# A fused stage's tail: a loop on PE for twelve groups, eight staging buffers, tables and paddings issued among them

## The reference, cut to what matters

```
x = x + tanh(g_xattn[0]) * attention0(layernorm(x), ctx)     # 16 heads
x = x + tanh(g_ffn[0])   * mixture_of_experts(layernorm(x))  # router, top 2 of 8 experts
Kp, Vp = ctx @ Wk + bk, tanh(ctx @ Wv + bv)                  # layer 1's keys and values
x = x + tanh(g_xattn[1]) * attention1(layernorm(x), Kp, Vp)
x = x + tanh(g_ffn[1])   * quantised_ffn(layernorm(x))
```

## Time and profile before

| what | value |
|---|---|
| three runs | 1030.18, 1034.2, 1043.85 us; median 1034.2 us |
| the profiled execution | 1035.45 us |
| its span, first to last instruction | 1033.6 us |
| granted clock of TensorE, mean | 0.840 of full |
| PE busy | 782.8 us (76%) |
| DVE, ACT, POOL busy | 731.4, 636.4, 610.2 us |
| DMA over the span | 132.16 MB, mean 128 GB/s |

### The profile page before, as it was taken

How to read it: one execution, slowest core, us unless ns; L and a number is a source line. 1 busy time by engine, 2 the same in 40 slices (tenths; PEclk the granted TensorE clock), 3 DMA queues, 4 the chain that set the end, 5 groups by cost and what they waited for, 6 DMA issues and landing times. The chain is left out here.

```text
span 1033.6 us, 19711 instructions
## 1 busy us (share of the span) xinstructions
PE 782.8 (76%) x6656; PEld 607.2 (59%) x6656; DVE 731.4 (71%) x1656; ACT 636.4 (62%) x1290; POOL 610.2 (59%) x617
## 2 busy tenths in 40 slices
PE   5389999988899889461499999999952798355355
PEld 3267767766676677350388888887741576322144
DVE  4776777877678874123287777777734798779988
ACT  5366666666667645251277777776741677489583
POOL 2145446878788886732057677776673884198500
PEclk9698988988889987785699999999985798767656
DMA  8123411122121214566667767676728533100013
GB/s 225 45 72 78 91 32 68 59 75 102 59 76 57 78 68 131 164 209 137 183 221 242 248 245 247 243 246 219 247 79 267 185 112 100 37 1 0 1 51 113
DMA packets 103827, 132.16 MB, mean 128 GB/s; under 512 B 23840, under 2 KB 78576, under 8 KB 97712
## 3 DMA queue, kind: packets, MB, share of 16 engines
q1 hardware_dynamic: 90240, 110.64, 33.8%
q0 software_dynamic: 9120, 18.91, 5.2%
q10 hardware_dynamic: 4368, 1.34, 0.9%
HBM read 86.59 MB, written 44.18 MB: 127 GB/s over the span
## 5 line engine op out<-in xcount | busy, mean ns | idle before, releaser
L1740 POOL DMA_INDIRECT m_results<-e_y,e_to x156 | 169.3, 1085 | 92.1 <-ACT e_y L1779 50.6
L324 POOL TENSOR_TENSOR a_probs<-a_probs,a_top 128x1024 f32<-128x1024 f32 x64 | 121.9, 1905 | 103.3 <-DVE a_top L958 100.6
L356 POOL DMA_INDIRECT m_tokens_to<-r_rows,r_place x128 | 128.4, 1003 | 46.5 <-issue 33.7
L1755 ACT ACTIVATE e_h<-e_ps_h,e_bias 128x512 f32<-128x512 f32 x156 | 107.6, 699 | 50.5 <-PE e_ps_h L1801 38.7
L1845 DVE TENSOR_TENSOR e_hp<-e_h,e_hp 128x512 fp32r<-128x512 f32 x156 | 108.2, 694 | 5.4
L1843 DVE CAST e_hp<-e_h 128x512 fp32r<-128x512 f32 x156 | 71.4, 458 | 52.9 <-ACT e_h L1755 38.4
L911 DVE TENSOR_TENSOR a_probs<-a_ps_s,a_mask 128x1024 f32<-128x1024 f32 x64 | 78.0, 1219 | 26.7 <-PE a_ps_s L548 26.2
L673 PEld LDWEIGHTS a_ps_o<-a_vals,a_probs_t 128*64 128x64 f32 x2048 | 74.6, 152 | 28.3 <-issue 27.7
L439 ACT ACTIVATE a_gated<-a_ps_o,tanh_gates 128x128 f32<-128x128 f32 x64 | 23.4, 365 | 101.3 <-PE a_ps_o L677 43.5
L673 PE MATMUL a_ps_o<-a_vals,a_probs_t 128*64 128x18 f32 x2048 | 81.4, 223 | 2.8 <-ACT a_heads_t L450 2.2
L694 PE MATMUL a_ps_pt<-ident,a_probs 128*128 128x128 f32 x512 | 81.6, 313 | 0.0
(11 more groups left out here) (291 smaller groups left out, 2018.3 us busy)
## 6 DMA issues: line engine op xcount, KB each, us to landing
e_weights<-m_weights_to SPq DMA_DIRECT2D x39, 1024.0 KB
e_rows<-m_tokens_to SPq DMA_DIRECT2D x39, 264.0 KB
a_ctx_in<-in_ctx_dram SPq DMA_DIRECT2D x32, 256.0 KB
m_weights_to<-r_parts SPq DMA_DIRECT2D x8, 1024.0 KB, 5.0
c_two<-m_results SPq DMA_DIRECT2D x3, 1536.0 KB, 15.3
m_keys_t<-n_keys SPq DMA_DIRECT2D x16, 256.0 KB
m_values<-n_values SPq DMA_DIRECT2D x16, 256.0 KB
c_keys_t<-m_keys_t SPq DMA_DIRECT2D x16, 256.0 KB, 2.6
```

Of the source, the lines that this page charges most:

```text
L324: pool.tensor_tensor(probs[:, j], probs[:, j], top[:, j].unsqueeze(2).broadcast_to([P, HEADS, SEQ]), ALU.subtract).then_inc(shifted, 1)
L356: pool.indirect_dma_start(tokens_to, bass.IndirectOffsetOnAxis(ap=place[:, k, q:q + 1], axis=0), rows[:, c % RING, q % CT, k, :], None).th ...
L1740: pool.indirect_dma_start(results, bass.IndirectOffsetOnAxis(ap=to[:, v, r:r + 1], axis=0), y[:, v, r], None).then_inc(sent[v], 16)
L1755: act.activation(h[:, c], ps_h[c][:], ACT.Gelu_apprx_tanh, bias=bias[:, n % ROWS, c:c + 1]).then_inc(h_sb, 1)
```

## The change

- The hand-written slots go. Contexts 0 to 3 stand in slots t = 64 to 67, the keys and values of groups 0 to 2 in slots 65 to 67. Groups 3 to 15 follow after the last slot: on PE the contexts 4 to 15 and the keys and values 3 to 14 in a `Fori` loop of three turns with four groups each, whose waits are computed from the loop's register; on ACT, DVE and SP as straight code.
- `keys1` and `values1` have eight buffers each, laid over `spread` and `probs`, and the waits for a store's landing are for the store eight groups earlier.
- On DVE `ends` is converted directly after the last places, then groups 3 to 5, then the tables, then groups 6 to 15.
- All eight paddings are issued by SP, one after the stores of each group from v = 5 on; ACT issues none.

```
@@ shapes @@
-    keys1 = sb("n_keys1", [P, 2, ST], F32)
-    values1 = sb("n_values1", [P, 2, QUAD, DM], F32)
+    keys1 = spread[:].rearrange("p u k t -> p (u k) t")
+    values1 = probs[:].rearrange("p j (h k) c -> p (j h) (k c)", h=2)
...
-    NEXT_SLOTS = (65, 66, 67, 69, 70, 71, 74, 75, 76, 78, 79, 80, 81, 82, 83, 84)
+    UNROLLED = 4
...
-        return NEXT_SLOTS.index(t) if t in NEXT_SLOTS else None
+        return t - TILES if TILES <= t < TILES + UNROLLED else None
@@ sync @@
             store_keys(v)
             if v:
                 store_values(v - 1)
+            e = v - UNROLLED - 1
+            if e == 0:
+                sp.wait_ge(ends_ready, 1)
+            if there(e, EXPERTS):
+                padding_of(sp, e)
         store_values(SUPERS - 1)
-        sp.wait_ge(ends_ready, 1)
-        for e in range(0, EXPERTS, 2):
-            padding_of(sp, e)
@@ scalar @@
-            if v >= 2:
-                act.wait_ge(keys_out[v % 2], 16 * (v // 2))
-            act.activation(keys1[:, v % 2], band(1), ACT.Identity, bias=bk1[:, 0:1]).then_inc(k1_sb, 1)
+            if v >= STAGED:
+                act.wait_ge(keys_out[v % STAGED], 16 * (v // STAGED))
+            act.activation(keys1[:, v % STAGED], band(1), ACT.Identity, bias=bk1[:, 0:1]).then_inc(k1_sb, 1)
...
+        for w in range(UNROLLED, SUPERS):
+            next_context(w)
+            next_keys(w - 1)
+        next_keys(SUPERS - 1)
         tanh_values(SUPERS - 1)
-        act.wait_ge(ends_ready, 1)
-        for e in range(1, EXPERTS, 2):
-            padding_of(act, e)
@@ tensor @@
+        def next_context(w, b, first=False):
+            if isinstance(w, int):
+                pe.wait_ge(loaded[b], 16 * ((SUPERS + w) // CTX_RING) + 16)
+            else:
+                pe.wait_ge(loaded[b], w * (16 // CTX_RING) + (16 * (SUPERS // CTX_RING + 1) - 16 // CTX_RING * b))
+            pe.wait_ge(s_sb, TILES) if first else pe.wait_ge(ct_sb, w + SUPERS)
...
+        with pe.Fori(0, (SUPERS - UNROLLED) // CTX_RING) as i:
+            for b in range(CTX_RING):
+                next_context(i * CTX_RING + (UNROLLED + b), b)
+                next_keys_values(i * CTX_RING + (UNROLLED + b - 1), (b + 1) % 2)
+        next_keys_values(SUPERS - 1, (SUPERS - 1) % 2)
@@ vector @@
+        def next_values(v):
+            dve.wait_ge(v1_ps, v + 1)
+            if v >= STAGED:
+                dve.wait_ge(values_out[v % STAGED], 16 * (v // STAGED))
+            dve.tensor_tensor(values1[:, v % STAGED].rearrange("p (k c) -> p k c", c=DM),
+                              band(2 + v % 2).rearrange("p (k c) -> p k c", c=DM),
+                              bv1[:].unsqueeze(1).broadcast_to([P, QUAD, DM]), ALU.add).then_inc(v1_raw, 1)
...
         dve.wait_ge(placed, PLACE_OPS * NCH)
         dve.tensor_copy(ends[:], total[0:1, :, 0]).then_inc(ends_ready, 1)
+        for v in range(UNROLLED - 1, UNROLLED + 2):
+            next_values(v)
         then(dve.tensor_tensor(count[:], total[:, :, 0], base[:], ALU.subtract))
...
         dve.tensor_copy(tables[0:1, 1], texp[0:1, :]).then_inc(tables_ready, 1)
+        for v in range(UNROLLED + 2, SUPERS):
+            next_values(v)
```

More of the change, by code:

```diff
@@ L44 @@
 CTX_RING = 4
+STAGED = 8
 FIRST = 3 * QUAD
@@ L115, in layer0 @@
     loaded = [sem(f"a_loaded{b}") for b in range(CTX_RING)]
-    keys_out, values_out = ([sem(f"n_{n}_out{u}") for u in range(2)] for n in ("keys", "values"))
+    keys_out, values_out = ([sem(f"n_{n}_out{u}") for u in range(STAGED)] for n in ("keys", "values"))
     (gates_in, q_in, k_in, w_in, ident_step, gates_ready, bq_set, own_set, stats1, step1, var_ready, std_ready,
@@ L191, in store_keys @@
             sp.wait_ge(k1_sb, v + 1)
-            sp.dma_start(g["keys_t"][:, ST * v:ST * v + ST], keys1[:, v % 2]).then_inc(keys_out[v % 2], 16)
+            sp.dma_start(g["keys_t"][:, ST * v:ST * v + ST], keys1[:, v % STAGED]).then_inc(keys_out[v % STAGED], 16)
         def store_values(v):
             sp.wait_ge(v1_sb, v + 1)
-            sp.dma_start(g["values"][:, QUAD * v:QUAD * v + QUAD, :], values1[:, v % 2]).then_inc(values_out[v % 2], 16)
+            sp.dma_start(g["values"][:, QUAD * v:QUAD * v + QUAD, :].rearrange("p k c -> p (k c)"), values1[:, v % STAGED])\
+                .then_inc(values_out[v % STAGED], 16)
         load_x(0)
@@ L256, in _ @@
                 store_values(v - 1)
+            e = v - UNROLLED - 1
[3 more added lines that the diff above has]
+                padding_of(sp, e)
         store_values(SUPERS - 1)
-        sp.wait_ge(ends_ready, 1)
-        for e in range(0, EXPERTS, 2):
-            padding_of(sp, e)
         sp.wait_ge(padded, 32 * PADDED)
         sp.wait_ge(weights_out, 16 * EXPERTS)
-        for u in range(2):
-            sp.wait_ge(keys_out[u], 16 * SUPERS // 2)
-            sp.wait_ge(values_out[u], 16 * SUPERS // 2)
+        for u in range(STAGED):
+            sp.wait_ge(keys_out[u], 16 * SUPERS // STAGED)
+            sp.wait_ge(values_out[u], 16 * SUPERS // STAGED)
     @block.gpsimd
@@ L415, in tanh_values @@
             act.wait_ge(v1_raw, v + 1)
-            act.activation(values1[:, v % 2], values1[:, v % 2], ACT.Tanh).then_inc(v1_sb, 1)
+            act.activation(values1[:, v % STAGED], values1[:, v % STAGED], ACT.Tanh).then_inc(v1_sb, 1)
         def next_context(v):
@@ L525, in _ @@
                     normalise(s + 2, (2, 3))
[L526 to L534, removed]
+                w = next_of(t)
+                if w == 0:
+                    act.wait_ge(kv_in, 64)
+                if w is not None:
+                    next_context(w)
+                    if w:
+                        next_keys(w - 1)
+        for w in range(UNROLLED, SUPERS):
+            next_context(w)
+            next_keys(w - 1)
+        next_keys(SUPERS - 1)
         tanh_values(SUPERS - 1)
-        act.wait_ge(ends_ready, 1)
-        for e in range(1, EXPERTS, 2):
-            padding_of(act, e)
     @block.tensor
@@ L578, in values, with next_keys_values @@
             mm.then_inc(v_ps, 1)
[L580 to L583, removed]
+        def next_context(w, b, first=False):
[4 more added lines that the diff above has]
+            pe.wait_ge(s_sb, TILES) if first else pe.wait_ge(ct_sb, w + SUPERS)
             for k in range(QUAD):
-                mm = pe.transpose(band(0)[:, P * k:P * k + P], ctx_in[:, n % CTX_RING, k, :], ident[:])
+                mm = pe.transpose(band(0)[:, P * k:P * k + P], ctx_in[:, b, k, :], ident[:])
             mm.then_inc(ct_ps, 1)
-        def next_keys_values(v):
-            pe.wait_ge(ct_sb, SUPERS + v + 1)
-            if v:
+        def next_keys_values(v, u):
+            pe.wait_ge(ct_sb, v + (SUPERS + 1))
+            if later(v, 1):
                 pe.wait_ge(k1_sb, v)
-            pe.matmul(band(1), wk1[:], context1[v % 2][:], start=True, stop=True).then_inc(k1_ps, 1)
-            if v >= 2:
+            pe.matmul(band(1), wk1[:], context1[u][:], start=True, stop=True).then_inc(k1_ps, 1)
+            if later(v, 2):
                 pe.wait_ge(v1_raw, v - 1)
             for k in range(QUAD):
-                mm = pe.matmul(band(2 + v % 2)[:, P * k:P * k + P], context1[v % 2][:, P * k:P * k + P], wv1[:],
+                mm = pe.matmul(band(2 + u)[:, P * k:P * k + P], context1[u][:, P * k:P * k + P], wv1[:],
                                start=True, stop=True)
@@ L723, in _ @@
                     transpose_x2(m)
[L724 to L732, removed]
+                w = next_of(t)
+                if w == 0:
+                    pe.wait_ge(kv_in, 64)
+                if w is not None:
+                    next_context(w, w, first=w == 0)
+                    if w:
+                        next_keys_values(w - 1, (w - 1) % 2)
+        with pe.Fori(0, (SUPERS - UNROLLED) // CTX_RING) as i:
[3 more added lines that the diff above has]
+        next_keys_values(SUPERS - 1, (SUPERS - 1) % 2)
     @block.vector
@@ L966, in _ @@
                     dve.memset(resets[:, :, 0], 0.0).then_inc(resets_set, 1)
[L967 to L976, removed]
+                w = next_of(t)
+                if w == 0:
+                    dve.wait_ge(kv_in, 64)
+                if w:
+                    next_values(w - 1)
         at = 0
```

## The result

The changed kernel took 1047.67 us (median of 20 runs, 1036.02 to 1055.65) against 1033.16 us for the kernel before (20 runs beside them): ratio 1.0158, 95% interval 1.0131 to 1.0186. That is 14.5 us slower, less than the 2% that I had called the bound of a difference, but clearly a loss, and outside my range of 1003 to 1043. The profiled execution took 1048.53 us with a span of 1046.8, so the two profiles stand 13.1 us apart. Ratios and intervals leave out runs more than 1.5% above the fastest of their kernel; medians and ranges take in all of them, so the two can differ slightly.

A forecast was written before the change was run, and what follows sets the result against it. Nothing saturated from 407 to 500 us; PE's completions came late during POOL's scatter runs. Start 421, groups partly late until 480.5, 4.5 landing, 2.3 barrier: first load 487.4, 11.7 earlier; 1035.45 - 11.7 = 1023.7, rounded to 1024; range 1003 to 1043.

The forecast's parts named there:

- the condition for late completions: Routing tail: PE's completions come late only when POOL's unbroken scatter run meets a full DMA as well.
- 421 to 431 at speed, 4.5 groups: Start of the group loop: 10 us without lateness, in which groups 3 to 7 pass.
- two episodes and one counterexample: Before's profile: completions 9 and 22 us late, then again, in POOL's long runs; PE unhindered at 602:619.
- 1.1 to 1.3 us: Loop from 431 to POOL's end at 461.5: time per PE record while late, so 30 us pass 1.7 groups.
- late from the first group: Slower rival: PE held from 421 to 461, two groups pass, first load 506.3, 1043 us; chance 0.15.
- makes PE or the queues late next, not POOL: Routing tail: closing POOL's 12.8 us gap ends its scatters at 460 instead of 473.9; POOL bounds no longer.
- the loop's start at 421: End of routing: router 15 2 us earlier, picks, counts and places 4 to 5 us, so groups start near 421.
- The loop at nothing: PE's engine loop over groups: its branches and register sums for waits add 0 us.
- The 17 us that I set beside it: PE's loop, upper bound: two taken backward branches wait 8.5 us each; the sum would be 1041 us.
- Staging at 0 to 3 us: Eight buffers for keys and values: remove 11.5 us of overlapping DVE store waits, worth 0 to 3 us.
- Tables: DVE's `ends` and tables move from after the last group to under the scatters; 8.4 us leave the end.
- the on-time rival: Completions on time in the tail: first load at 470.2, 28.9 us gained, 1007 us; chance 0.38.

The follow-up runs named there:

- e8: Changed kernel with GpSimd waiting after every four of the last 38 scatters until these have landed, late job; 1023.46 us, 0.9911 of before.
- late job: Second follow-up job, where completions came late with long remote waits; the kernel before took 1031.92 us there.
- e13: The kernel before itself, unchanged, traced in one of the on-time jobs; 1000.84 us in its one run.
- e1: Changed kernel with TensorE's engine loop written out as straight code, on time; 1004.71 us, 1.0043 of before.
- e14: The changed kernel itself, as control in one of the on-time jobs; 1006.61 us, 1.0040 of before.
- e10: Changed kernel with GpSimd waiting for the landing after every eight of the last scatters, on time; 1009.90 us, 1.0099 of before.
- e12: Changed kernel with the landing wait after every eight scatters and the loop written out as straight code, on time; 1007.79 us, 1.0073 of before.
- e7: Kernel before with eight staging buffers laid over `spread` and `probs`, nothing else, late job; 1033.18 us, 0.9992 of before.
- e3: Changed kernel with the tables moved ahead of the value adds of groups 3 to 5, on time; 1006.63 us, 1.0061 of before.
- e5: The kernel before itself, unchanged, traced in the late job; 1037.43 us in its one run.
- e6: The changed kernel itself, as control in the late job; 1048.62 us, 1.0123 of before.
- e2: Changed kernel with the eight paddings back at the end, four on SP and four on ACT, on time; 1011.92 us, 1.0112 of before.
- e4: Changed kernel with paddings back at the end on two queues and tables ahead of the value adds, on time; 1007.65 us, 1.0074 of before.
- on-time jobs: The four follow-up jobs in which no kernel had long remote waits; before took 1001.8, 1001.5, 1002.6 and 999.5 us.
- e9: Kernel before with GpSimd waiting for the landing after every four of the last 38 scatters, on time; 1022.12 us, 1.0203 of before.
- e16: Kernel before with eight staging buffers and a plain 1.2 us GpSimd write after every four scatters, on time; 1004.59 us, 1.0028 of before.
- e18: Repeat of e16 in another on-time job, kernel before with staging and plain writes; 1003.50 us, 1.0038 of before.

## Why the prediction was wrong

*The step that failed* is the condition for late completions: "They need a full DMA too, as I read it", and from it "421 to 431 at speed, 4.5 groups". The trace after has a DMA share of 0.26 from 412 to 418 and of 0.16 where the lateness begins:

```profile
421.00:429.00 8.00, 4.50 (x16) 3.34 (x17) 3.72 (x20) 2.01 (x4) 6.17 (x7) 0.50 0.16 52
429.00:443.00 14.00, 3.21 (x16) 2.33 (x14) 0.69 (x1) 0.00 (x0) 10.58 (x12) 0.74 0.35 110
```

Here the values of the loop's first group were already late by 8 us, so of the 4.5 groups that I let pass at speed not one had its values through by 431. I had inferred a second cause from two episodes and one counterexample. The counterexample, 602:619, is 12 scatters in 17 us, 1.4 us each, with one of POOL's casts after every four; that it was looser than the tail's run was in the trace too, and I took the DMA share for the difference. It is also a sign that fours with a short pause between them, and no wait for a landing, can pass in a late execution; it is another stage with another load, so it is no proof. The price of my lateness was shaky too: "1.1 to 1.3 us" a record is a mean over 24 us in which the records came in bursts, and 4.5 and 1.7 groups leave 6.8 of thirteen, where the sum has six.

*What took its place* is the third case, "late from the first group", to which I gave 0.15, with 506.3 for the first load and 1043 us. It let the lateness begin 6 us into a run, and the first late completion came at 16; else its mechanism is what happened, and its terms can be held against the trace. Groups 5 to 15 start at 466.2, not 461.5 (4.7 late: completions come back 5.6 us after the run's end, not at it). From there to the last store's issue at 505.7 it is 39.5 us, not 37: SP's pace with a padding is 4.4 us, not 3.8. A padding takes 2.7 us in place of 2.45, since the value load has a median of 0.92 us where before it had 0.62, and the three issues beside it take 1.7 us in place of 1.4 (0.64, 0.50 and 0.43 against 0.47, 0.32 and 0.32). PE's four waits for contexts come of it. The end takes 5.5 us, not 7.8. Together +4.9, 511.2. Of the loss against before, then, the late completions are the larger part: 14.5 us in all, 4 us without them (1.0158 and 1.0123 against 1.0040), so some 10. The traces agree: from the run's first scatter to the first load the late executions take 86.7 and 87.1 us before and 98.3 and 98.4 after, 11.5 apart, against 4.2 on time. And e8 shows it from the other side, 25 us from nothing but breaks in POOL's run.

*The stall that I counted as a gain was PE's chance.* I wrote that POOL's gap of 12.8 us goes and "makes PE or the queues late next, not POOL". On a late job that gap, 440 to 453, and the first microseconds of the next run are when before's completions arrive and its groups 8 to 14 pass, most of them at 2.2 us each. The change closed it. That the gap is what ended the lateness is argued from these times and from e8, where breaks do it; no run put the gap alone back. e13 adds that before has the gap only because of the lateness: on time its 38 scatters make one run too.

*The other steps.* The scatters from 412 to 460 in one run of 38: right (412.8 to 460.6). `ends` near 425: right, 425.43. But the loop's start at 421 was 3.8 us early: router 15 is recorded at 417.38 and not at 415.7 to 416.7, DVE's picks start at 419.27, and PE waits for the places until 424.76, where the granted clock is 0.50. The loop at nothing: right, by e1 beside e14, by e10 beside e12 and by the 2.18 us across a turn. The 17 us that I set beside it were a misreading of the rule: the Trainium skill, "Runtime: NRT & Kernel Launch", section "Instruction fetch mechanics", has a taken branch wait only where its target lies outside a window of two blocks of 256 instructions. A turn of this loop shows 56 matmuls and as many weight loads, so by my estimate from these its start is still inside; these runs neither bear the rule out nor contradict it. Staging at 0 to 3 us: not contradicted, by the ratio 0.8 us gained with an interval of 4.4 gained to 2.9 lost (e7). Tables: I had them "under the scatters" and 8.4 us off the end; they stood behind three adds that were late, ran from 467.4 to 475.9 and so were under nothing. On time they hold PE for 4.3 us (e14, 4.5 in e1), and yet e3, which takes them away from there, is 1.9 us slower than e1: SP's pace covers them. The sum for the on-time rival gave a first load at 470.2 and 28.9 us of gain. On time the changed kernel's first load is at 475.9, near it; the gain is not there because before's own is at 470.6. I had charged the late completions to the kernel before as its property, when another execution of it runs without them.

*What stays open:* what in POOL's run holds TensorE's work back, how long or how dense a run may be (fours with a wait between have no wait for a remote release over 2.7 us, 15 in a row have one of 11.4), whether a pause does as well as a landing, and why some jobs show it and others don't. I didn't try the scatters on another engine.

## What to carry to other kernels

A wait that ends with no instruction of the core is a question, not an idle gap to be filled: ask what ran throughout it, and what ended with it, before moving work there. In some executions an unbroken run of GpSimd's scatters held back the completions of TensorE: a few passed during it, the rest and the full pace came with its end or with a stall in it. So a change that makes such a run longer should be tried with breaks in the run as well, and be timed in several jobs, since breaking has a price where nothing is late: 0.2 to 0.6% for the changed kernel with the looser breaks, 2% for the kernel before with a wait after every four. Against it stands what the lateness costs in the tail, some 24 us before and 31 us after the change (e5 and e6 beside e13 and e14). And where two parts of a change cover each other, take them out together as well as singly (e2, e3, e4).

## What was not expected of the hardware

- Completions of PE up to 34 us late (group 4's value matmuls, recorded until 432.2, released DVE at 466.20) while GpSimd issued 38 scatters, one each 1.26 us, at a DMA share of 0.16 to 0.35; the same waits to 0.1 us in two executions; down to 2.7 us when the scatters came four at a time with a wait for their landing. The Trainium skill, "SBUF — State Buffer", section "Who interferes with whom", says "PE and ACT never wait on anyone", of the ports to SBUF. Taken as a rule for TensorE beside a busy GpSimd this trace doesn't agree: its DRAIN of 9.69 us against 0.47 shows it late with its own work. Whether a port has to do with it no run tells.
- The same program runs 3% faster where this is absent (before: 999.5 to 1002.6 us in four jobs, 1031.9 and 1033.2 in the other and in the first measurement); in two single executions that stand 36.6 us apart (e5 and e13) 24.1 us lie in the tail, between the run's first scatter and the first load, 5.8 ahead of it and 6.7 in the later stages. The paced kernel of the late job, e8, still takes 5 us longer behind the first load than the changed kernel on time, so a late job loses something outside the tail too; what it is I didn't follow.
- A register load from `ends` (SP's TENSOR_LOAD) took 0.50 to 1.00 us, median 0.92, when stores and context loads stood around it, 0.48 to 0.78, median 0.62, in the kernel before, and 0.27 us for the tables in the next stage.
- Four paddings on each of two queues, issued together at the end, leave SP waiting 9.1 to 12.5 us for the last to land in the on-time jobs (e2, e4, e9, e13, e16, e18) and 8.5 us in the first profile; spread over the groups they leave 2.2 to 3.7 us for the last stores (e14, e1).
